# A decoder's retention layer: keys and values of batch 0 before the last turn, decay tables in the experts' search, two norms in one, the next norm begun early

## What is computed

```python
x = x + _L0_ffn_ref(_layernorm(x), ...)        # 8 experts, top 2, capacity 154
x = x + _L1_attn_ref(_layernorm(x), W_qkv, W_o, log_gamma)
x = x + _L1_xattn_ref(_layernorm(x), ctx_512, ...)

def _L1_attn_ref(x, W_qkv, W_o, log_gamma):    # the retention
    qkv = (x @ W_qkv.T).reshape(b, L, 3, H, dk)
    q, k, v = (qkv[:, :, 0], qkv[:, :, 1], qkv[:, :, 2])
    k = _layernorm(k)                          # over the 16 of a head
    gamma = jax.nn.sigmoid(log_gamma)
    def step(S, qkv_t):
        S = gamma * S + v_t[..., :, None] * k_t[..., None, :]
        return S, jnp.einsum('bhde,bhe->bhd', S, q_t)
    ...
    return y @ W_o.T

def _L1_xattn_ref(xx, ee, ln1_g, ln1_b, ln2_g, ln2_b, ...):
    x = _ln(xx, ln1_g, ln1_b)                  # xx is itself a layernorm
    x = x + _mha(x, x, ...)                    # "a1": starts with one more _ln
    ...
```

## Time and profile before

| | |
|---|---|
| median of 3 runs | 1726.13 us (1725.15 to 1732.22) |
| the profiled execution, its own time | 1727.11 us |
| its span on the core | 1725.4 us |
| granted TensorE clock, mean | 0.946 |
| TensorE busy | 1547.7 us, 90% |
| VectorE, ScalarE, GpSimd busy | 50%, 40%, 33% |

### The profile page before, as it was taken

One profiled execution on the slowest core, in us unless ns is written; L12 is line 12 of the kernel. 1 busy time (PEld: TensorE's weight loads), 2 busy tenths in 40 slices (PEclk: granted clock), 3 DMA queues, 4 the chain that ended last, 5 costly groups with the idle time before them and its releaser, 6 DMA issues.

```text
span 1725.4 us, 24218 instructions
## 1 busy us (share of the span) xinstructions
PE 1547.7 (90%) x9690; PEld 821.5 (48%) x9703; DVE 858.5 (50%) x1829; ACT 688.4 (40%) x1010; POOL 572.2 (33%) x688
## 2 busy tenths in 40 slices
PE   8999989999999877995776999899899999995997
PEld 5788953333333353773452333357233333563565
DVE  2255558599846562102575267324677774212221
ACT  3434223566654422221514445532255556421211
POOL 3043232500125503003201255651167778603000
PEclk9999999999999988997887899999799999996999
DMA  6000010000000049341004000040200000282000
GB/s 194 1 1 1 1 46 6 1 1 1 1 1 1 1 159 314 109 158 53 4 2 55 0 1 1 25 134 29 88 1 1 2 1 25 76 309 99 26 11 8
DMA packets 70339, 84.24 MB, mean 49 GB/s; under 512 B 24945, under 2 KB 55889, under 8 KB 69202
## 3 DMA queue, kind: packets, MB, share of 16 engines
q1 hardware_dynamic: 67395, 75.31, 13.6%
q0 software_dynamic: 2832, 7.38, 1.3%
HBM read 63.56 MB, written 19.51 MB: 48 GB/s over the span
## 4 chain that ended last, share of the span: by engine, by line
PE 79%; DVE 8%; ACT 4%; issue 3%; DMA 3%; POOL 2%; SPq 0%; DVEq 0%; POOLq 0%; ACTq 0%
PE psum L1278 12%; PE psum L1297 9%; PE psum L1250 6%; PE psum L3123 5%; PE psum L2459 3%; PE psum L657 3%; PE psum L2466 3%; PE psum L1274 3%; PE psum L1319 3%; PE psum L2065 3%; DVE a_nm L1370 3%; PE psum L1424 3%; PE psum L3144 2%; PE psum L2057 2%; PE psum L686 2%
## 5 line engine op out<-in xcount | busy, mean ns | idle before, releaser
L1370 DVE TENSOR_REDUCE a_nm<-psum 128x1 f32<-128x512 f32 x384 | 249.2, 685 | 136.8 <-PE psum L1250 76.4
L1370 DVE TENSOR_REDUCE xa_nm<-psum 128x1 f32<-128x512 f32 x256 | 161.9, 683 | 27.8 <-PE psum L1250 22.6
L1332 ACT ACTIVATE a_w<-psum 128x1024 f32<-128x1024 f32 x112 | 109.0, 1021 | 87.2 <-PE psum L1278 71.7
L1332 ACT ACTIVATE xnT<-psum 128x1024 f32<-128x1024 f32 (+3 forms) x104 | 94.8, 952 | 82.1 <-PE psum L1278 72.9
L1278 PE MATMUL psum<-xa_cq,xa_ckT 32*128 32x512 f32 x512 | 104.1, 587 | 0.0
L1250 PE MATMUL psum<-a2kr,a2qr 32*128 32x512 bf16 x256 | 87.1, 405 | 14.8 <-DVE a_nm L1370 13.6
L1278 PE MATMUL psum<-a2qT,a2kT 32*128 32x512 f32 x512 | 98.4, 607 | 0.0
L1175 POOL TENSOR_TENSOR a_w<-a_w 128x512 f32<-128x512 f32 x60 | 76.3, 1271 | 16.1 <-PE psum L1297 9.9
L3123 PE MATMUL psum<-sw_wv,sw_xgT 128*128 x176 | 79.9, 608 | 0.4 <-issue 0.3
L1250 PEld LDWEIGHTS psum<-a2kr,a2qr 32*128 32x128 bf16 x256 | 21.1, 92 | 121.6 <-DVE a_nm L1370 111.8
L1332 ACT ACTIVATE xn<-psum 128x1024 f32<-128x1024 f32 (+3 forms) x64 | 56.5, 922 | 47.2 <-PE psum L1278 43.5
(11 more groups left out here) (528 smaller groups left out, 3273.5 us busy)
## 6 DMA issues: line engine op xcount, KB each, us to landing
mo_w<-in_L_ffn_W SPq DMA_DIRECT2D x16, 1024.0 KB, 7.6
sw_wv<-in_L_ffn_w_v SPq DMA_DIRECT2D x4, 2048.0 KB, 17.7
scratch_a2v<-co_v SPq DMA_DIRECT2D x16, 256.0 KB
scratch_a2k<-co_k SPq DMA_DIRECT2D x16, 256.0 KB
a2kT<-scratch_a2k SPq DMA_DIRECT2D x8, 512.0 KB, 8.1
a2v<-scratch_a2v SPq DMA_DIRECT2D x4, 1024.0 KB, 11.2
sw_wp<-in_L_ffn_w_proj SPq DMA_DIRECT2D x4, 1024.0 KB, 20.0
a1li<-in_L_xattn_a_li_w SPq DMA_DIRECT2D x2, 1024.0 KB, 5.5
```

Of the source, the lines that this page charges most:

```text
L1332: e.activation(self.weights(n, c)[:, 2 * jj:2 * jj + 2, lo:S], ps[:, pr:pr + 2, lo:S], ACT.Exp, scale=self.scale).then_inc(*self.weighed.m ...
L1370: e.tensor_reduce(self.nm[n % 3][:, q, part, h:h + 1], view, AX.X, ALU.max, negate=True).then_inc(*self.max_taken.mark(*i))
```

## The change

- **Keys and values early.** TensorE multiplies keys and values of chunks 0 to 3 between `Turn` 0 and `Turn` 1 of the experts' last norm (`tensor_early`, called through `rows.between`). ScalarE copies two of them before and two after the root and apply of norm 4 to 7 (`scalar_early`). `Turn` 0 is now copied by ScalarE alone.
- **Tables in the search.** The GpSimd iotas, the VectorE steps (`vector_gamma`, one or two small instructions in rounds 1, 2, 4 to 7) and the ScalarE exponentials (`scalar_tables`, after the copies of step 2 and of steps 4 to 9) stand in the experts' search. The load of `log_gamma` is issued after that of the router's bias. The cut of `decay` (L2690) follows the scatter on GpSimd. The clearing of `v` goes from GpSimd to VectorE (`vector_zero`), before the gathered rows are added.
- **Two norms folded.** The plain norm and the one with `ln1_g`, `ln1_b` become one with `twice=True`: the variance v enters as v(1 + e) + e*e. Chunks 4 and 5 are done by VectorE in two instructions each; the six others ("b") by ScalarE (normed) and then GpSimd (times gain, plus shift).
- **Next norm ahead.** a1's norm of chunks 0 to 3 is taken inside the retention's rows 5 and 6, and its `Turn` 0 stands before rows 7. `Turn` 1 stands in a1's lead-in behind the fourth query; norm 4 to 7 of a1 follows the first key and query on ScalarE.
- **Smaller moves.** ScalarE and TensorE turn the keys (m, 0) before key norm 1. a1's weights are issued at the retention's start. A filler tile `above` keeps them apart from the retention's tiles.

```diff
--- before.py
+++ after.py
...
+        if self.twice:
+            e.tensor_scalar(self.std[:, four, 0], self.agg[:, four, 1], 1.0 + LN_EPS, LN_EPS * LN_EPS, ALU.mult, ALU.add).then_inc(
...
+            if self.of(c) == "b":
+                w.wait_ge(*self.scaled.at(self.name, c))
+                w.wait_ge(*step.now())
+                e.tensor_tensor(dst, dst, self.gain, ALU.mult).then_inc(*step.mark())
+                w.wait_ge(*step.now())
+                e.tensor_tensor(dst, dst, self.shift, ALU.add).then_inc(*self.by["b"].mark(self.name, c))
...
+        if self.scalar_between and c == NC - 1:
+            self.scalar_between(e, w, 0)
         if c % 4 == 3:
             self.norm.scalar_root(e, w, c - 3)
             self.norm.scalar_apply(e, w, c - 3)
+        if self.scalar_between and c == NC - 1:
+            self.scalar_between(e, w, 1)
         if self.turn and c >= NC - 2:
             self.turn.scalar_copies(e, w, c - (NC - 2))
-        if self.next and c == 3:
+        if self.next and c == self.ahead_at:
...
+        self.turn.all_by_scalar = (0,)
         self.rows = Rows(k, "mo_rows", k.x, k.x, self.norm, self.turn, gathered=True)
+        self.rows.between, self.rows.scalar_between = retention.tensor_early, retention.scalar_early
...
+        self.retention.sync_gamma(e)
...
+        self.retention.pool_distances(e, w)
...
+        self.retention.pool_cut(e, w)
...
             self.operands.scalar_step(e, w, i)
+            self.retention.scalar_tables(e, w, i)
...
+        self.retention.vector_zero(e, w)
         added = self.rows.added
         for c in range(NC):
...
+        self.retention.vector_gamma(e, w, i)
...
+            self.norm = Norm(k, pre + "_norm", xb, core, "vava", mem=mem) if cross else norm
...
+            pieces[8:8] = [("turn", 1)]
+            pieces[2:2] = [("root", 4), ("apply", 4)]
             pieces += [("value_rows", c) for c in range(NC)]
-            return [("root", 0), ("root", 4), ("apply", 0), ("apply", 4), ("turn", 0), ("turn", 1)] + list(self.attention.lead_in(pieces, 3))
+            return list(self.attention.lead_in(pieces, 5))
...
-            self.sync_projections(e)
...
-            self.vector_norm(e, w, 0)
+            w.wait_ge(*self.k.vec.now())
         self.vector_norm(e, w, 4)
-        for g in (4,) if self.cross else (0, 4):
-            self.norm.vector_apply(e, w, g)
+        self.norm.vector_apply(e, w, 4)
...
-        self.norm = Norm(k, "re_norm", k.x, k.xn, "vava", mem=mem)
-        self.first_norm = double.first_norm
+        self.norm = Norm(k, "re_norm", k.x, k.xn, "bbbbvvbb", double.da_rows[:, 0, :], double.da_rows[:, 1, :], mem=mem, twice=True)
         self.rows = Rows(k, "re_rows", k.x, k.x, self.norm)
-        self.set = k.by_pool("re_set")
-        self.gamma, self.tables = k.by_vector("re_gamma"), k.by_scalar("re_tables")
+        self.rows.ahead_at = 6
...
-        yield from (("keys_values", c) for c in range(SC))
         yield "key_norm", 0
         yield from (("queries", (m, 0)) for m in range(FC))
         yield from (("keys_values", c) for c in range(SC, NC))
+        yield from (("key_turn", (m, 0)) for m in range(FC))
         yield "key_norm", 1
-        yield from (("key_turn", (m, 0)) for m in range(FC))
         yield from (("queries", (m, 1)) for m in range(FC))
...
+            if c == NC + 1:
+                yield "turn_ahead", 0
...
+            elif step == "rows" and i % 4 == 3:
+                w.wait_ge(self.double.rows_load.sem, 64)
+                self.norm.pool_apply(e, w, i - 3)
...
+    def tensor_early(self, e, w):
         for f in range(FC):
             w.wait_ge(*self.centred.at(f))
             w.wait_ge(*self.weights_ready.at(f, 0))
             w.wait_ge(*self.weights_ready.at(f, 3))
+        for c in range(SC):
+            self.tensor_keys_values(e, w, c)
...
+            elif step == "turn_ahead":
+                self.rows.next.xturn.tensor(e, w, i, self.ring)
...
+    def scalar_tables(self, e, w, i):
+        lg, tables = self.lg, self.tables
+        if i == 2:
+            w.wait_ge(*self.gamma.at("minus_abs"))
+            e.activation(lg[:, 2, :], lg[:, 1, :], ACT.Exp).then_inc(*tables.mark("exp"))
+            w.wait_ge(*tables.now())
+            e.activation(lg[:, 3, :], lg[:, 2, :], ACT.Ln, bias=1.0).then_inc(*tables.mark("ln"))
+        for h in range(3 * (i - 4), min(H, 3 * (i - 3))) if 4 <= i else ():
+            w.wait_ge(*self.set.at("distance"))
+            w.wait_ge(*self.gamma.at("log"))
             m, t, j = self.place(h)
             e.activation(self.decay[:, t, j, :], self.dist[:, :], ACT.Exp, scale=lg[:, 0, h:h + 1]).then_inc(*tables.mark("decay", h))
...
+        if i == 9:
+            w.wait_ge(*self.gamma.at("to_end"))
...
+    def scalar_early(self, e, w, half):
+        for c in (2 * half, 2 * half + 1):
+            self.scalar_keys_values(e, w, c)
...
+    def vector_zero(self, e, w):
+        e.memset(self.v[:, :, :, :], 0.0).then_inc(*self.zeroed.mark())
...
     def vector_rows(self, e, w, c):
-        if c == 0:
+        self.rows.vector_add(e, w, c)
+        if c == NC - 1:
             w.wait_ge(self.double.rows_load.sem, 64)
-        self.rows.vector_add(e, w, c)
         self.rows.vector_norm(e, w, c)
-        if c % 4 == 3:
-            for i in range(c - 3, c + 1):
-                w.wait_ge(*self.norm.done(i))
-                self.first_norm.vector_stats(e, w, i)
-            self.first_norm.vector_variance(e, w, c - 3)
-            self.first_norm.vector_apply(e, w, c - 3)
```

180 lines of the change are left out of this document (95 added, 85 removed).

## The result

The changed kernel took 1705.9 us (median of 4, 1696.82 to 1708.43), the kernel before, on the same chip, 1728.7 (1725.15 to 1732.22): 0.9859 of the time, 95% interval 0.9814 to 0.9904 (the ratios here and below are taken over the runs; the two medians alone give 0.9868). All runs told of here were fast but one, of "GpSimd second" (1753.7 us, in the chip's slow state), which is left out. The forecast was 1698 with a range of 1690 to 1710. The profiled execution has a span of 1706.7, 18.7 less than before.

The account below looks back on a forecast made before the run. It took a chain of hand-overs between engines, not TensorE's work, as the bound. 6.0 + 1.5 - 0.5 + 0 + 6.6 + 15.4 - 0.9 = 28.1 us gained, forecast 1698 us, range 1690 to 1710.

Parts of the forecast that it names:

- Part 1: Retention's start: keys and values of batch 0 between the turns, queries earlier; gain 6.0 us, between 1.0 and 8.2.
- Part 2: Before the first scores: without tables, ScalarE's copies follow TensorE more closely; gain 1.5 us, between 0.5 and 2.5.
- The tables in the search: Experts' search: table work moved there is mostly hidden, round 4 not stalled; charged 0.5 us, at most 3.
- Clearing of `v`: Before the gathered rows are added: VectorE's clearing takes 4.3 us within its idle time; costs nothing, at worst 2.2 us.
- Part 3: Retention loop's middle: no norm work left on VectorE after the scales, next decay directly behind; gain 6.6 us, called firm.
- Part 4: Loop's tail, from that decay to a1's first key projection: 15.6 us where it took 31.0; gain 15.4, between 10 and 16.5.
- Part 5: a1's lead-in: norm of chunks 4 to 7 fits by 2 us; loss 0.9, from loss 4.5 to gain 0.7.
- The norm's second half holds a1: Rival at a1's lead-in: slow GpSimd work makes the second norm late; gain 19.1 us, time 1707, chance 0.14.
- The early matmuls all at 1.2 GHz: Rival on the early keys and values: Part 1 gives only 1.0, sum 23.3 us, time 1703, chance 0.10.
- The lower clock into a1: Rival at a1's start: clock at 0.50 for 20 us costs 10 us; time 1708, chance 0.10.
- slower: Whole kernel slower than before, if a1's lower-clock stretch is longer than 56 us; chance 0.03.
- Its signs of being wrong: First keys only after 820, first maxima waiting for a1's statistics, or clock after 892 at 0.50 for over 15 us.

Follow-up runs that it names:

- GpSimd second: Changed kernel with the folded norm of chunks 4 and 5 moved from VectorE to ScalarE and GpSimd; 1707.3 us, ratio 0.9879 to the kernel before.
- keys behind: Changed kernel with keys and values of batch 0 put back behind both turns; 1712.5 us, ratio 0.9901 to the kernel before.
- tables back: Changed kernel with decay tables, VectorE's small steps and GpSimd's cut back at the retention's head; 1705.2 us, ratio 0.9861 to the kernel before.
- run again: The same changed kernel in a later execution, nothing edited; 1703.7 us, ratio 0.9852 to the kernel before.
- three moves: Changed kernel with batch 1's turn two pieces earlier, batch 0's turn in banks 0 and 1, a1's ring begun at bank 2; 1696.7 us, ratio 0.9815.

## Why the prediction was right, and where it was off

The mechanisms came as forecast but for the fit of a1's lead-in, and the range held the time; the forecast itself was 7.9 us too low, and the gain by the medians of one chip was 22.8 us against the 28.1 of the sum. The parts missed by up to 3 us each, in both directions; that the misses cancelled in part is luck. In its own steps:

- **Part 1**, 6.0: measured 6.7 to the queries, 7.1 when undone. The estimate between the two clock levels (10 us) met the 9.57.
- **Part 2**, 1.5: 2.4 behind Part 1 in the profile, 5.4 when undone. I had counted only the lag of ScalarE's copies in the old order. With the keys early, 11.6 us of tables would have been the next bound, so the two parts are worth less by themselves than undoing each shows. From the last copy to the scores it is 56.4 us with neither, 54.4 with Part 2 alone (keys behind), 52.7 with Part 1 alone (tables back) and 47.3 with both: 2.0 and 3.7 alone, 9.1 together, 5.4 and 7.1 as the last to come (the kernel before lacks the smaller moves as well).
- **The tables in the search**, 0.5: not more than 0.6, the spread of that stretch, and round 4 stood where it did (326.2 us behind the first cut before, 326.6 after, 326.0 again). By the Trainium skill (ScalarE: Activation LUTs, section What ACT_TABLE_LOAD costs) each switch has a drain of 1.38 us on top; the four loads shown have their next instruction 0.01 to 0.02 us behind them, so that it isn't seen here.
- **Clearing of `v`**, nothing: 3.47 us, where the forecast took 4.3, a figure that no row of the kernel before gives; it was over 1.06 before the first row; GpSimd issued a gather at 803.53, inside it. The Trainium skill (SBUF — State Buffer, section Who interferes with whom) doesn't count a memset among what blocks GpSimd on trn2, and the row agrees.
- **Part 3**, 6.6: from the first scores to that decay 32.6 us in place of 37.4, 4.8. VectorE's work is gone as counted, but the loop now has two stretches at 1.2 GHz, about 850 to 857 and 864 to 867, where before it had one. The run with the tables back, with one such stretch there, has its decay at 30.6: 6.8 earlier, the forecast's figure.
- **Part 4**, 15.4: 15.3. Its parts were less exact: GpSimd took 0.73 and not 0.9 an instruction, and the turn, having both banks of the rows, held them for 1.1. Only the turn's place was undone (1.7 us); that the norm taken ahead gives the rest is read from the trace.
- **Part 5**, a loss of 0.9 with "It fits by 2 us": this is the step that failed. From a1's first key to its first exact score it was 4.0 us longer than before in the profile and 8.1 when run again. In the run again VectorE ends the norm of chunks 4 to 7 at 24.6 after the decay (23.5 in the forecast), and TensorE, with its first projections at the full clock but for 1.0 us, has the first scores for the maxima at 23.1, where I had the maxima at 25.5: the norm is 1.0 late, not 2 early. I had counted the clock as a gain of 1.0 in this part. In the run again it was the larger loss: 18.1 us of the lead-in were at 1.2 GHz, where the kernel before had 5.0, and from the first maxima to the transposed ones it took 30.0 in place of 23.3. Further: in the first profile 1.0 for the turned copies and a projection of 3.38 in place of 1.88 behind that pause, and in both 0.84 for a bank that two more openings had moved on to the last value row. The three moves bring the same stretch to 54.5 us, 1.7 below the kernel before: the loss was one of order, not of work.
- **The rivals.** The norm's second half holds a1: true, by 1.0 us, where I had priced 9, and not because GpSimd was slow. The early matmuls all at 1.2 GHz: no, they took 9.57 us (its 23.3 us should be 23.1 by the sum's own terms). The lower clock into a1: a1's way to its output was 2.4 us longer than before in the first profile and 1.8 shorter in the next, so chance; but in the lead-in it cost, 34.7 and 38.8 against 29.9 in the three profiles that had none of it there, though these have the moves too, so that the clock's share of the difference isn't shown. The kernel is nowhere near slower.
- **Its signs of being wrong.** The first keys started at 816.7 on the time base of before (821.16 less 4.5), ahead of 820. The other two came true: the first maxima waited for the norm in the run again, and behind a1's first key the clock was at 1.2 GHz for over 15 us in both profiles, for 35 and 32 up to a1's output, where the kernel before had 22.

The rest of the gap is the start: in the first profile 5.5 us went in code that didn't change. Without it the profile gives 18.7 + 5.5 = 24.2 against the sum's 28.1. By stretches, measured less forecast: search and experts +1.5, scores +1.6, loop and tail -1.9, lead-in -3.1, a1 -2.4 and the rest +0.3.

## What to carry to other kernels

When work is taken out of a chain of hand-overs, price the next one again: the gain of each edit depends on which of the others stand. Where a stage is entered earlier, its fit has to be counted at the fastest that its other side can be, not at what it was when both were late. And where a turn or a product is moved, count the banks that it opens: it takes them from what is queued right behind it, and it shifts the ring for all that comes later.
